# Second attention stage: scores from high and low parts in three passes from the second batch on

## The reference, cut to what matters

```python
q = (x @ W_q).reshape(b, n, HEADS, DIM_HEAD)            # 8 heads of 64, 224 queries
k = (context @ W_k).reshape(b, j, HEADS, DIM_HEAD)      # 750 keys
v = (context @ W_v).reshape(b, j, HEADS, DIM_HEAD)
sim = jnp.einsum('bihd,bjhd->bhij', q, k) * scale
sim = jnp.where(mask[:, None, None, :], sim, max_neg)
attn = jax.nn.softmax(sim, axis=-1)
out = jnp.einsum('bhij,bjhd->bihd', attn, v).reshape(b, n, INNER)
return out @ W_o + b_o
```

## Time and profile before

| | |
|---|---|
| time, median of 3 runs | 3227.76 us (3226.5 to 3231.46) |
| time of the profiled execution | 3229.13 us |
| its span | 3227.3 us |
| second stage | about 768 to 1875 us |
| PE busy in the span | 3018.3 us (94%) |
| DVE busy in the span | 1646.6 us (51%) |
| ACT busy in the span | 1348.0 us (42%) |
| mean granted TensorE clock | 0.970 |

### The profile page before, as it was taken

One profiled execution on the slowest core, in us unless ns is written; L12 is line 12 of the kernel. 1 busy time (PEld: TensorE's weight loads), 2 busy tenths in 40 slices (PEclk: granted clock), 3 DMA queues, 4 the chain that ended last, 5 costly groups with the idle time before them and its releaser, 6 DMA issues. The chain is left out here.

```text
span 3227.3 us, 50841 instructions
## 1 busy us (share of the span) xinstructions
PE 3018.3 (94%) x19312; PEld 2477.8 (77%) x19312; DVE 1646.6 (51%) x3608; ACT 1348.0 (42%) x2298; POOL 700.2 (22%) x721
## 2 busy tenths in 40 slices
PE   5889998978999999999999949999999999999997
PEld 4667777756788777778777738888888888888886
DVE  5888888873556556666566633333333333333321
ACT  5677777764555555555555511111111111111111
POOL 0000000011111221112121033243434343434332
PEclk9889999989999999999999969999999999999999
DMA  3011111123111111111111022141313131313122
GB/s 100 24 35 44 37 45 45 46 82 121 42 50 38 45 38 56 51 38 42 41 52 34 25 74 75 54 97 55 96 55 96 56 95 56 95 57 94 57 71 37
DMA packets 93875, 189.72 MB, mean 59 GB/s; under 512 B 17568, under 2 KB 27552, under 8 KB 91712
## 3 DMA queue, kind: packets, MB, share of 16 engines
q1 hardware_dynamic: 79168, 158.68, 16.1%
q0 software_dynamic: 14592, 29.43, 5.1%
HBM read 140.25 MB, written 47.82 MB: 58 GB/s over the span
## 5 line engine op out<-in xcount | busy, mean ns | idle before, releaser
L1777 ACT ACTIVATE f_hf<-f_h 128x448 f32<-128x448 f32 x256 | 139.4, 544 | 1014.1 <-PE f_h L1804 958.0
L1748 DVE CAST f_hh<-f_hf 128x448 fp32r<-128x448 f32 x256 | 105.9, 414 | 847.0 <-ACT f_hf L1777 822.0
L1819 PE MATMUL f_y<-f_w2h,f_hh 128*128 128x512 f32 x896 | 357.5, 399 | 0.0
L1819 PE MATMUL f_y<-f_w2h,f_hl 128*128 128x512 f32 x896 | 354.0, 395 | 0.0
L1819 PE MATMUL f_y<-f_w2l,f_hh 128*128 128x512 f32 x896 | 352.2, 393 | 0.0
L1707 POOL TENSOR_TENSOR f_w1l<-f_raw,f_w1h 128x512 fp32r<-128x512 f32 x128 | 182.4, 1425 | 778.6 <-DVE f_w1h L1731 778.5
L1396 ACT ACTIVATE c_s_sb<-c_s_sb,c_nmx 112x750 f32<-112x750 f32 x256 | 236.1, 922 | 159.6 <-DVE c_nmx L1239 156.6
L1388 ACT COPY c_pT<-psum 125x672 f32<-125x672 f32 x256 | 184.6, 721 | 224.3 <-PE psum L1496 223.2
L1804 PE MATMUL f_h<-f_xTh,f_w1h 128*128 128x448 f32 x1024 | 255.2, 371 | 2.9 <-DVE f_xTl L1736 1.4
L1496 PEld LDWEIGHTS psum<-a_ident,c_s_sb 112*125 112x125 f32 x1536 | 193.5, 189 | 79.9 <-issue 76.2
L1804 PE MATMUL f_h<-f_xTl,f_w1h 128*128 128x448 f32 x1024 | 250.7, 366 | 0.0
(11 more groups left out here) (252 smaller groups left out, 5766.6 us busy)
## 6 DMA issues: line engine op xcount, KB each, us to landing
f_raw<-in_w SPq DMA_DIRECT2D x128, 512.0 KB, 4.2
h_craw<-in_ctxT SPq DMA_DIRECT2D x16, 1125.0 KB, 5.1
a_x_in<-in_x SPq DMA_DIRECT2D x9, 896.0 KB, 5.5
a_xr<-in_x SPq DMA_DIRECT2D x8, 896.0 KB, 6.0
x_dram<-a_xr SPq DMA_DIRECT2D x8, 896.0 KB, 4.8
q_dram<-a_q SPq DMA_DIRECT2D x32, 224.0 KB, 5.4
h_q<-q_dram SPq DMA_DIRECT2D x16, 448.0 KB, 5.4
c_x<-x_dram SPq DMA_DIRECT2D x16, 448.0 KB, 4.9
```

What stands on the lines that cost most here:

```text
L1748: dve.tensor_copy(hs[0][:, l % 2, c * HC:c * HC + HC], hf[:, c, :]).then_inc(h_hi, 1)
L1777: act.activation(hf[:, c, :], H[:, 0:HC], ACT.Gelu_apprx_tanh).then_inc(free, 1)
L1819: mm = pe.matmul(Y[t][:], hs[a][:, l % 2, 128 * t:128 * t + 128], w2s[b][:, l % NSLOT, :], start=j == 0 and q == 0, stop=last_of_expert(l) ...
```

## The change

Five things change, all in the second stage:

1. The keys are kept as two F32R tensors, `kT_hi` (in the place of `kT`) and `kT_lo`, and the queries as `q_hi` (in the place of `q`) and `q_lo`. The low parts lie where the first stage had its rows and work tiles.
2. ACT writes the high part of a K unit from PSUM where it wrote the F32 keys before, and raises `keys_hi` in the place of `gen_free`. It writes the high part of the queries where it copied them before, and raises `queries_hi` in the place of `q_made`.
3. DVE makes the low part of each K unit (`lo_of_keys`: PSUM less the high part, one subtraction), and only that frees the bank. For units of slots 1 and 2 it stands one step later, between `normalise` and `masked`; for units of slot 0 in the same step behind `masked`; for K(3,0) at the end of the step loop's body.
4. DVE makes the low part of the queries, in two halves, at steps 9 and 15 behind `masked` (`lo_of_queries`), and that raises `q_made`.
5. `scores` issues twelve F32R matmuls (three products x two halves of the keys x two heads) in the place of four F32 ones, for every batch but the first.

```diff
@@ Handover
+        self.kT_over = Region(nc, "c_", sb.at, sb.end)
         self.kT = sb("kT", [128, H2 // 2, J])
...
-        self.q2, self.q = sb("q2", [128, KC, T]), sb("q", [128, KC, T])
+        self.q2 = sb("q2", [128, KC, T])
+        self.q_over = Region(nc, "c_", sb.at, sb.end)
+        self.q = sb("q", [128, KC, T])
@@ self_attention
+    handover.low = Region(nc, "c_", sb.at, sb.at + 2 * TPI * C * 4)
@@ cross_attention
+    kT_part = [handover.kT_over("kT_hi", [128, H2 // 2, J], F32R)[:], handover.low("kT_lo", [128, H2 // 2, J], F32R)[:]]
+    q_part = [handover.q_over("q_hi", [128, KC, T], F32R)[:], handover.low("q_lo", [128, KC, T], F32R)[:]]
@@ DVE
+        def lo_of_keys(i, kind, unit):
+            dve.wait_ge(keys_hi, number(SPLIT, i, kind, unit) + 1)
+            (hi, lo), src = unit_places(kind, unit)
+            dve.tensor_tensor(lo, src, hi.bitcast(F32), ALU.subtract).then_inc(gen_free[BANK[kind, unit]], 1)
+
+        def lo_of_queries(i, g):
+
+            dve.wait_ge(q_hi, i * 2 + g - 1)
+            pair = slice(2 * g, 2 * g + 2)
+            dve.tensor_tensor(q_part[1][:, pair], q2[:, pair], q_part[0][:, pair].bitcast(F32), ALU.subtract).then_inc(q_made, 1)
@@ DVE body
                     normalise(*step(i, s + 1))
+                for unit in (projections(kind, s - 1, (1, 2)) if s else []):
+                    if unit[0] == "K":
+                        lo_of_keys(i, kind, unit)
                 if has_step(kind, s + 2):
                     masked(*step(i, s + 2))
+                for unit in projections(kind, s, (0,)):
+                    lo_of_keys(i, kind, unit)
+                if s in (9, 15) and kind != "last":
+                    lo_of_queries(i + 1, s // 10)
                 if kind != "first":
                     tail(i, kind, s)
+            if kind != "last":
+                lo_of_keys(i, kind, K(3, 0))
@@ ACT
         def copy_queries(i, g):
             act.wait_ge(q_loaded, i * 16 + 16)
-            act.copy(q[:, 2 * g:2 * g + 2], q2[:, 2 * g:2 * g + 2]).then_inc(q_made, 1)
+            pair = slice(2 * g, 2 * g + 2)
+            if isinstance(i, int) and i == 0:
+                act.copy(q[:, pair], q2[:, pair]).then_inc(q_made, 1)
+            else:
+                act.copy(q_part[0][:, pair], q2[:, pair]).then_inc(q_hi, 1)
...
-            act.copy(dst, src).then_inc(gen_free[BANK[kind, unit]], 1)
+            if unit[0] == "K":
+                act.copy(dst[0], src).then_inc(keys_hi, 1)
+            else:
+                act.copy(dst, src).then_inc(gen_free[BANK[kind, unit]], 1)
@@ PE
-            for a in range(2):
-                for e in range(2):
-                    rows = slice(64 * e, 64 * e + 64)
-                    j0 = a * (J - HW)
-                    mm = pe.matmul(scb[e][0:R, a, 0:HW], q[rows, m, t0:t0 + R], kT[rows, m, j0:j0 + HW],
-                                   start=True, stop=True, tile_position=(64 * e, 0))
+            native = isinstance(i, int) and i == 0
+            parts = [(q, kT)] if native else [(q_part[x], kT_part[y]) for x, y in ((0, 0), (0, 1), (1, 0))]
+            for n, (queries, keys) in enumerate(parts):
+                for a in range(2):
+                    for e in range(2):
+                        rows = slice(64 * e, 64 * e + 64)
+                        j0 = a * (J - HW)
+                        mm = pe.matmul(scb[e][0:R, a, 0:HW], queries[rows, m, t0:t0 + R], keys[rows, m, j0:j0 + HW],
+                                       start=n == 0, stop=n == len(parts) - 1, tile_position=(64 * e, 0))
```

More of the change, by code:

```diff
@@ L1011, in unit_places @@
         if what == "K":
-            return handover.key_places(bank(kind, unit), m, a)
+            j0, width = (0, KEY_SPLIT) if a == 0 else (KEY_SPLIT, J - KEY_SPLIT)
+            return [part[:, m, j0:j0 + width] for part in kT_part], bank(kind, unit)[:, 0:width]
         return v[:, 2 * a:2 * a + 2, 256 * m:256 * m + 256], bank(kind, unit)[0:JB].rearrange("p (b c) -> p b c", b=2)
@@ L1029, in cross_attention @@
     xn_stored, out_stored = sem("xn_stored"), sem("out_stored")
-    q_made, mb_made = sem("q_made"), sem("mb_made")
+    q_hi, q_made, mb_made, keys_hi = sem("queries_hi"), sem("q_made"), sem("mb_made"), sem("keys_hi")
     gen_full = sem("gen_full")
```

## The result

The changed kernel takes 3244.85 us (median of 5 runs, 3240.25 to 3247.0) against 3230.28 of the kernel before (5 runs); the ratio is 1.0047, 95% interval 1.0032 to 1.0061. It is slower by half a per cent, as forecast (3240, and slower at 0.74). The profiled execution took 3247.0 us.

What follows compares the result with a forecast made beforehand. PE was taken to bound the batch loop. Gains of 2.1 against waits of 3.1 gave +0.93 us a batch, +13.0 over fourteen; with +0.5 first and -1.2 last, +12.3, median 3240 us, range 3218 to 3262.

Steps and rivals of the forecast that it cites:

- The block: One scores block on PE: three F32R passes take 1.20 to 1.21 us in place of 1.46, saving 0.25.
- 2-4, 4-6, 12-14: PE's time between these scores blocks: no low part stands where PE waits, so -0.25 us each.
- Both rivals on PE: Scores: heads not side by side, block 0.77 longer, 3364, chance 0.04; or weight loads show, block 1.7, 3300, chance 0.04.
- upper bound of the gain: Scores block: saves 0.29 us if pairs of matmuls follow at 0.16, half of 0.32.
- The row of the K units: F32R matmuls over the same 376 columns, one every 0.17 us; taken as the new scores' pace, giving 0.25.
- 6-8, 8-10, 10-12: PE's time between these scores blocks: waits behind low parts add 0.21, 0.80 and 0.79 us.
- 0-2: PE from S0 to S2: V(1,0) waits 0.52 for the bank that K(3,1)'s low part frees; +0.27 us.
- the walk: Pair-by-pair account of one batch, placing each low part and PE's waits; sum +0.93 us a batch.
- 12-14 and 14-0: PE from S12 to S0: -0.25 us with no low part in the way, then -0.39 as S0's mask comes earlier.
- The sum: All eight pairs of a batch: gains of 2.1 against waits of 3.1, +0.93 us; fourteen batches +13.0.
- The first and the last batch: First pays for low parts in 6-8 and 8-10, +0.5 us; last makes only K(3,1), -1.2 us.
- The whole: Whole kernel +12.3 us: 3241.4 profiled, 3240 for the median, 0.4% slower.

Runs made afterwards that it cites:

- Experiment 3: Changed kernel with shorter low parts of the keys, 188 columns each, and all three products reading high parts only; 3228.44 us, ratio 0.9991.
- experiment 2: Changed kernel with the low parts alone: made but not read, scores one F32 product as before; 3266.59 us, ratio 1.0117.
- Experiments 4 to 7: Four runs moving the router's exponential or low parts of keys, the third on the kernel before, the others on the changed one; 3243.75, 3232.59, 3230.59, 3240.15 us.
- experiment 4: Changed kernel, router's bank first: in step 11 the low part of K(1,1) goes behind the two instructions freeing that bank; 3243.75 us, ratio 1.0039.
- experiment 5: Changed kernel, router early: ACT's exponential of the logits ahead of its copies, low part of K(1,1) behind DVE's twelve router instructions; 3232.59 us, ratio 1.0004.
- the passes alone: Changed kernel without low parts: all three F32R products read the high parts; 3211.6 us, ratio 0.9945.
- two moves: Changed kernel with the low part of K(1,1) behind the router's bank-freeing instructions and that of K(2,0) behind the mask in step 12; 3240.15 us, ratio 1.003.
- heads in turn: Changed kernel with all six scores matmuls of one head written before those of the other; 3297.17 us, ratio 1.0206.
- experiment 6: Kernel before the change with only ACT's exponential of the router's logits moved ahead of its copies; 3230.59 us, ratio 0.9998.
- all moves: Changed kernel with keys' low parts where DVE idles, queries' low parts on POOL, and the router's exponential ahead of ACT's copies; 3207.91 us, ratio 0.9921.

## Why the prediction was right, and where its steps were not

- **The block.** From 1.46 to 1.20 or 1.21 by the forecast, from 1.45 to 1.22 as measured; the pairs with nothing in their way (2-4, 4-6, 12-14) gained 0.24 or 0.25. Both rivals on PE are out: the heads go side by side, and no load shows. The prediction's upper bound of the gain, 0.29, was added up wrong: two pair-widths of 0.16 are 0.32. The row of the K units, which it went by, was the right one.
- **6-8, 8-10, 10-12.** Forecast 6.53, 9.10 and 10.55; measured 6.55, 9.10 and 10.59. Experiment 3 shows that the length of the subtraction sets them, experiment 2 that they are there without the passes too.
- **0-2.** Forecast +0.27, measured +0.11: 9.33. The low part of K(3,1) frees the bank at 1272.62, 6.96 behind S0 where the walk had 7.12. The mechanism was right, its size 0.16 too large: of that 0.09 is the overlap of two DVE instructions in a row, which the prediction had read from the earlier trace rows and left out between this normalisation and the low part, and 0.05 is DVE's delay, 1.00 (1268.33 - 1265.66 against 1255.63 - 1253.96) where the walk had 1.05.
- **12-14 and 14-0: right numbers, incomplete reason.** The prediction said of the router's chain that it "ends before the next normalisation needs it only a little later than S12, as before", and let 12-14 and 14-0 gain on their own. Experiments 4 to 7 show that two chains lead from S10 to S0 and are about equally long. The one from ACT's exponential through DVE's router, left alone by experiment 4, gives 26.25; with both removed (experiment 5) it is 25.07; and the wait for K(2,0)'s bank adds 10.59 - 9.52 = 1.07 to that, 26.14, though no run has it alone. The forecast of the change was not touched by it; a forecast of its repair was, and the one on record for experiment 4 missed. The same chain is why the passes alone gained 1.41 and not the 2.1 of the prediction's own gains: S0 followed the exponential by the same 16.2 us as before the change. So the -0.39 of 14-0 came out in the changed kernel only because the wait at K(2,0) hid the router's chain; taken as a statement on that chain, it was wrong.
- **The sum.** +0.85 a batch against +0.93. Over the 14 batches +10.67 and not +11.9, because the kernel before has two batches of 68.69 among them: its copy behind ACT's jump came 3.47 behind S0 in them (2.40 to 2.77 in the other twelve), and the pair 0-2 took 9.87. The prediction had said that the loop repeats to some 0.01 us; in two of 14 it doesn't.
- **The first and the last batch.** Forecast +0.5 and -1.2, measured 73.97 - 69.85 = +4.1 and 58.01 - 56.73 = +1.3. Most of the miss lies in two stretches where the granted clock differs. The stretches of the kernel before, from S0 to S4 of the first batch and from S8 to S10 of the last:

```profile
783.36:800.04 16.68, 13.28 (x90) 11.30 (x89) 8.74 (x20) 9.60 (x18) 7.91 (x5) 0.90 0.45 180
1833.23:1841.50 8.27, 8.02 (x52) 5.47 (x52) 5.54 (x14) 4.56 (x9) 0.00 (x0) 0.79 0.18 55
```

The same two of the changed kernel:

```profile
786.49:806.23 19.74, 14.74 (x89) 11.53 (x89) 10.33 (x20) 9.61 (x18) 7.60 (x5) 0.79 0.36 142
1849.87:1860.64 10.77, 10.61 (x56) 8.05 (x56) 5.79 (x14) 5.22 (x10) 0.00 (x0) 0.54 0.27 78
```

And the first in the kernel with two moves, which changes nothing there:

```profile
783.35:798.48 15.13, 11.71 (x89) 9.73 (x88) 8.74 (x20) 9.54 (x17) 7.91 (x5) 1.00 0.51 203
```

  The first stretch holds no low part that PE waits for, and its time goes with the clock, but not with it alone: 15.1 us at 1.00 and 16.6 to 16.7 at 0.87 to 0.90, but at 0.79 to 0.81 it is 17.7 to 18.0 in four kernels (low parts alone, shorter low parts, heads in turn, router early) and 19.7 in three (changed, passes alone, router's bank first). The timeline of the changed kernel shows what these three have more:

```profile
793.03 2.35 POOL L1159 TENSOR_TENSOR c_x<-c_x,c_bo 112x1024 f32<-112x1024 f32 x1
793.10 2.69 DVE L1232 TENSOR_SCALAR c_s_sb<-c_s_sb,c_rec 112x750 f32<-112x750 f32 x1
...
796.70 0.97 PE L1524 MATMUL psum<-h_kT,h_q 64*112 64x376 f32 x2 [5.00 <-DVE c_mx L1242]
```

  DVE's normalisation starts 0.07 behind an addition of POOL's and takes 2.69, and S2 waits 5.00 for the mask behind it. In the kernel before it starts earlier, at 788.73, takes 1.62, and is done before that addition starts at 789.90; S2 waits 3.40. These 1.6 us and the lower clock are the 3.1 of the first stretch; since the passes alone show 19.7 too, the low parts aren't its cause. The pairs 6-8 and 8-10 of the first batch give +0.8, where the low parts are. Without its pair 8-10 (10.77 at a mean clock of 0.54, against 8.27 at 0.79) the last batch is 1.2 shorter, as forecast. Nearly so low a clock is seen there without any part of the change: the kernel of experiment 6 takes 10.54 at 0.58 for that pair, and of those with three passes the one with shorter low parts takes 7.84 and the one with all moves 7.82, at 0.78.
- **The whole.** The difference of the two spans, 17.8, is +10.7 in the 14 batches, +4.1 in the first, +1.3 in the last, and +2.8 - 1.1 ahead of the second stage's first block and behind its last, in code that didn't change. The medians differ by 14.6, forecast 12.3. That the total came so near is in part luck: in the profiled pair the 14 batches came out 2.3 under the forecast 13.0 and the rest 7.9 over it.

## What to carry to other kernels

A shorter matmul on the engine that bounds a loop pays only if what it asks of its neighbours fits between their waits: here the passes gave 1.41 us a batch, the subtractions took 2.26. In other places they took 0.43: against the passes alone, 8-10 is 0.32 longer and 0-2 0.11, and the others are no longer. (The sums, 66.37 against 66.63, flatter them, since the early router took 0.68 from 14-0 and the passes alone don't have it; that kernel with the early router wasn't run.) Moving work to an idle engine isn't free either, if it slows the one that it was taken from. Before trusting the repair of one wait, follow the other engines from the same point to the next place where all meet, and compare the lengths: two chains may be equally long, and the trace names only the one that ended last. An instruction that frees a bank, or that starts a long chain elsewhere, belongs ahead of work that merely has to be done at some time.

## What the runs showed of the hardware that I had not expected

- Matmuls on the two halves of the rows overlap without being written alternately: with the heads in turn PE began the second head 0.44 us behind the first, inside its run of six, and the block took 1.66 and not 2.2.
- ACT's first instruction behind its loop's jump came up to 3.7 us behind the jump (1258.92 to 1262.58), 2.13 of them idle; in the changed kernel the copy comes 1.7 behind the jump and is never late. Within a kernel the copy comes at a few distances from S0, not spread evenly: 2.40, 2.74 and 3.47 before the change, 3.15 and 3.84 with the early router. The Trainium skill (Runtime: NRT & Kernel Launch, Instruction fetch mechanics) says that a taken branch to code outside the fetched window stalls until that code is fetched. The delay behind the jump fits that; no run shows a fetch. Why a loop of 120 recorded instructions is late in some kernels and batches and not in others stays open, and putting 64 or 128 instructions ahead of it didn't make the batches alike.
- VectorE's normalisation, 0.61 us by itself, took 1.02 to 1.31 in all 28 cases where GpSimd's subtraction of 1.15 ran beside it (all moves), and 2.69 beside GpSimd's addition of 2.35 (793.10, changed kernel).
- In the first batch of the stage, S0 to S4 took 15.1 us at a mean granted clock of 1.00, 16.6 to 16.7 at 0.87 to 0.90 and 17.7 to 19.7 at 0.79 to 0.81, that is with more or less of it at the lower of the two levels, though PE's work there is the same.
